# Graph layer with adjacency masks: products for two units at a time, one row step, the first x ahead of the first adjacency unit

## The reference

```python
masks = (relation[None] == rel_ids[:, None, None, None])      # rel_ids = 1..4
h = einsum('rbnm,bmd->rbnd', masks, x)
y = einsum('rbnd,rdo->bno', h, weight) + bias
out = layernorm(x + y, axis=-1, eps=1e-5)
```

## Time and profile before

| | |
|---|---|
| median of 3 runs | 120.71 us |
| the profiled execution | 120.54 us |
| its span, first to last instruction | 118.8 us |
| TensorE clock granted, mean | 0.985 |
| busy: PE, weight load, DVE, ACT, POOL | 106.6, 80.4, 84.8, 88.1, 70.3 us |
| 32 checks (L522) | 1994 ns each |
| 64 masks (L699) | 687 ns each |
| weight loads of the products (L619) | 98 ns each |
| x_lo on POOL (L448), one batch | 2144 ns |
| one row normalised on POOL (L488) | 457 ns |
| combining one row of statistics (L717) | 154 ns |
| DMA | 42.22 MB, mean 355 GB/s |

### The profile page before, as it was taken

How to read it: one execution, slowest core, us unless ns; L and a number is a source line. 1 busy time by engine, 2 the same in 40 slices (tenths; PEclk the granted TensorE clock), 3 DMA queues, 4 the chain that set the end, 5 groups by cost and what they waited for, 6 DMA issues and landing times.

```text
span 118.8 us, 2879 instructions
## 1 busy us (share of the span) xinstructions
PE 106.6 (90%) x1012; PEld 80.4 (68%) x1023; DVE 84.8 (71%) x252; ACT 88.1 (74%) x114; POOL 70.3 (59%) x132
## 2 busy tenths in 40 slices
PE   6788999899999979999999999999999999999400
PEld 2168898799997646767676767676868676679300
DVE  1055678397877848696959887787779777998840
ACT  4088277947797999799999499968987698925530
POOL 2007001940047998399569955995689577977740
PEclk9999999999999999999999999999999999999985
DMA  3999999999999999999999999999999999450271
GB/s 73 389 408 411 414 407 422 414 391 412 425 414 384 419 403 436 380 414 414 419 391 404 422 406 394 420 406 423 377 433 411 415 399 383 141 177 0 85 248 35
DMA packets 12419, 42.22 MB, mean 355 GB/s; under 512 B 882, under 2 KB 7155, under 8 KB 8947
## 3 DMA queue, kind: packets, MB, share of 16 engines
q1 hardware_dynamic: 12256, 41.49, 88.6%
q10 hardware_dynamic: 146, 0.52, 1.3%
HBM read 37.81 MB, written 4.19 MB: 354 GB/s over the span
## 4 chain that ended last, share of the span: by engine, by line
PE 58%; DMA 29%; SPq 5%; DVE 2%; issue 1%; ACT 0%; DVEq 0%
PE h_ps L619 32%; DMA adj_sb<-adj 29%; PE ids_t L601 16%; PE y_ps L633 9%; SPq L396 4%; PE ids_t L633 1%; DVE x_sb L758 0%; SPq L393 0%; SPq L412 0%; ACT std L539 0%; DVE stats L711 0%; DVE x_sb L705 0%; DVE moments L717 0%; DVEq L255 0%; DVE shift L751 0%
## 5 line engine op out<-in xcount | busy, mean ns | idle before, releaser
L522 ACT ACTIVATE junk<-adj_sb,minus 128x2048 bf16<-128x2048 int32 x32 | 63.8, 1994 | 0.4 <-DMA adj_sb<-adj 0.4
L699 DVE TENSOR_SCALAR mask_t<-ids_t 128x1024 bf16<-128x1024 uint16 x64 | 43.6, 687 | 25.2 <-PE ids_t L601 24.1
L601 PEld LDWEIGHTS ids_t<-ident,adj_sb 128*128 128x128 bf16 x512 | 36.5, 123 | 13.8 <-DMA adj_sb<-adj 2.7
L601 PE MATMUL ids_t<-ident,adj_sb 128*128 128x128 bf16 x512 | 40.0, 221 | 2.3 <-DMA adj_sb<-adj 2.2
L619 PE MATMUL h_ps<-mask_t,x_lo 128*128 128x512 bf16 (+2 forms) x184 | 33.5, 314 | 0.0
L619 PE MATMUL h_ps<-mask_t,x_hi 128*128 128x512 bf16 (+2 forms) x173 | 31.1, 310 | 1.2 <-DVE mask_t L699 0.6
L448 POOL TENSOR_TENSOR x_lo<-x_sb,x_hi 128x1024 f16<-128x1024 f32 x7 | 15.0, 2144 | 24.2 <-ACT x_hi L531 24.2
L488 POOL TENSOR_SCALAR x_sb<-x_sb,rstd,shift 128x128 f32<-128x128 f32 x55 | 24.0, 457 | 1.0
L535 ACT ACTIVATE h_all<-h_ps 128x512 f32<-128x512 f32 (+2 forms) x23 | 10.6, 463 | 18.1 <-PE h_ps L619 18.1
L454 POOL TENSOR_TENSOR x_sb<-x_sb,bias_sb 128x1024 f32<-128x1024 f32 x8 | 19.0, 2377 | 7.8 <-DVE x_lo L764 7.7
L619 PEld LDWEIGHTS h_ps<-mask_t,x_hi 128*128 128x128 f16 x184 | 15.6, 98 | 7.2 <-DVE mask_t L699 1.2
(11 more groups left out here) (44 smaller groups left out, 30.8 us busy)
## 6 DMA issues: line engine op xcount, KB each, us to landing
adj_sb<-adj SPq DMA_DIRECT2D x27, 1024.0 KB, 19.5
...
bias_row<-bias ACTq DMA_DIRECT2D x1, 0.5 KB
```

The costliest lines, as they stand in the source:

```text
L522: nc.scalar.activation(junk[:, at % 2], adj_sb[:, slot, 2 * k:2 * k + 2, :], ACT.Square, scale=2.0, bias=minus[:, 0:1], accum_out=squares[ ...
L601: last = nc.tensor.transpose(bank[:, j, :], words[:, j // step(b), j % step(b), 0, :], ident[:, :])
L699: nc.vector.tensor_scalar(mask_t[:, b % 2, :, u * P:(u + 1) * P], ids_t[u % T_BANKS][:, :, :].bitcast(UINT16), 1.0, None, ALU.mult).then_i ...
```

## The change

- Every batch but the last is split into groups of four units. Products are issued for two units at a time (256 columns), first with x_hi, then with x_lo; in batch 0's first group for one unit at a time. Transposes run between them: in a group's first half those of its own third and fourth unit, in its second half the first two of the next group. The group before is projected after the first half. The last batch stays 4, 2, 1, 1.
- All batches have row step 2. Batch 1 is loaded in single units.
- x of batch 0 is loaded by SP's queue, in two halves ahead of unit 0; ACT's queue only has the bias row. x of later batches moves ahead of the last pair of the batch before.
- DVE's and ACT's orders are rewritten for it. DVE sums the group one back. ACT checks two pairs a group (three in two groups) and makes x_hi after the first check.
- End: x is added to the last unit's projection on PE, by a product with an fp32 identity (`add_x`); its statistics and its normalising read PSUM. Only the rows that ACT normalises have a shift. Of the rows of the last 16 units POOL normalises 3 + 2 + 2 (4 + 2 + 1 before), ACT 5 + 2 (4 + 2 + 1), DVE the last 2.
- The second pass is rewritten in short loops over single units.

```diff
-    def step(b):
-        return J if b < EARLY else 2
+    S = 2
...
-        if b == 0:
-            return [(0, 1), (1, 1), (2, 2), (4, 2), (6, 2)]
-        if b == 1:
-            return [(0, 2), (2, 2), (4, 2), (6, 2)]
         return [(0, 4), (4, 2), (6, 1), (7, 1)] if b == B - 1 else [(0, 4), (4, 4)]
...
-        return b == 0 or (b == 1 and u < 2)
+        return b < EARLY
...
-        first = [1, 2, 2, 3, 4, 5, 6, 7, 8, 11, 13]
+        first = [2, 4, 6, 8, 10, 12, 15]
         if g.index < len(first):
             return first[g.index]
-        return min(PAIRS * (g.b + 1) + (2 if ends_batch(g) else 0), PAIRS * B)
+        return min(2 * g.index + 4, PAIRS * B)
...
+            for n in range(2):
+                sp.dma_start(units_of(x_sb[:, 0], n * HALF, HALF), rows_of(x, 0, n * HALF, HALF)).then_inc(s_x0[n], 16)
             load_unit(0, 0)
             load_unit(0, 1)
             sp.dma_start(w_sb[:, 0, :], weight[0]).then_inc(s_w, 16)
             for u in range(2, J):
                 load_unit(0, u)
-            load_unit(1, 0)
             load_x(1)
-            load_unit(1, 1)
-            for k in range(1, PAIRS):
-                load_adj(1, k)
-            load_x(2)
+            for u in range(J):
+                if u == 6:
+                    load_x(2)
+                load_unit(1, u)
             for b in range(EARLY, B):
                 for k in range(PAIRS):
+                    if k == PAIRS - 1 and b + 1 < B:
+                        load_x(b + 1)
                     load_adj(b, k)
-                if b + 1 < B:
...
-            normalise(full, full.units[:4])
+            normalise(full, full.units[:3])
             roots(ra)
             normalise(ra, ra.units[:2])
-            normalise(rb, rb.units[:1])
+            normalise(rb, rb.units[:2])
...
-            act.dma_start(units_of(x_sb[:, 0], 0, 0, J), rows_of(x, 0, 0, J)).then_inc(s_x[0], 16)
             act.dma_start(bias_row[:, :], bias.rearrange("(a d) -> a d", a=1)).then_inc(s_bias, 16)
             act.preload_act_table(ACT.Sqrt)
-            split_hi(0, slice(0, HALF), s_hi0)
-            split_hi(0, slice(HALF, J), s_hi)
+            split_hi(0, slice(0, HALF), s_x0[0], s_hi0)
+            split_hi(0, slice(HALF, J), s_x0[1], s_hi)
+            act.wait_ge(s_const, 1)
+            check(0, 0)
             act.wait_ge(s_spread, 1)
             nc.scalar.activation(bias_sb[:, :], y_ps[:, 0, :], ACT.Copy).then_inc(s_biased, 1)
-            act.wait_ge(s_const, 1)
-            check(0, 0)
+            check(0, 1)
             for g in groups[1:LAST]:
-                b = g.b
                 copy_h(groups[g.index - 1])
-                if ends_batch(g):
-                    split_hi(b + 1, slice(0, J), s_hi)
-                todo = range(pairs_checked_by(groups[g.index - 1]), pairs_checked_by(g))
-                for n, at in enumerate(todo):
+                for n, at in enumerate(range(pairs_checked_by(groups[g.index - 1]), pairs_checked_by(g))):
                     check(at // PAIRS, at % PAIRS)
-                    q = groups[g.index - 2] if g.index >= 2 else None
-                    if n == 0 and q and ends_batch(q):
-                        root(sets[q.b])
+                    if n == 0 and ends_batch(g):
+                        if g.b:
+                            root(sets[g.b - 1])
+                        else:
+                            continue
+                        split_hi(g.b + 1, slice(0, J), s_x[g.b + 1], s_hi)
+                if g.index == 1:
+                    split_hi(1, slice(0, J), s_x[1], s_hi)
...
-            normalise(full, full.units[4:5])
+            normalise(full, full.units[3:4])
             copy_h(e)
             root(ra)
-            normalise(full, full.units[5:7])
+            normalise(full, full.units[4:6])
             copy_h(d)
-            normalise(full, full.units[7:]).then_inc(s_aside, 1)
+            normalise(full, full.units[6:]).then_inc(s_aside, 1)
             root(rb)
             normalise(ra, ra.units[2:]).then_inc(s_aside, 1)
-            normalise(rb, rb.units[1:2]).then_inc(s_aside, 1)
...
-            def products(g, n, of):
-                todo = [(j, part) for part in (x_hi, x_lo) for j in range(J)]
-                lo, hi = len(todo) * n // of, len(todo) * (n + 1) // of
-                if n == 0:
-                    pe.wait_ge(s_mask, unit_no(g.b, g.units[-1]) + 1)
+            def products(g, units, part):
+                if part is x_hi:
+                    pe.wait_ge(s_mask, unit_no(g.b, units[-1]) + 1)
                     if g.index:
                         pe.wait_ge(s_hi, g.b + 1)
-                    if g.index >= 2:
+                    if g.index >= 2 and units[0] == g.first:
                         pe.wait_ge(s_h, g.index - 1)
-                if lo <= J < hi and g.index:
+                elif g.index:
                     pe.wait_ge(s_lo, g.b + 1)
-                for j, part in todo[lo:hi]:
-                    if g.index == 0 and j % HALF == 0:
+                to = slice((units[0] - g.first) * P, (units[-1] + 1 - g.first) * P)
+                cols = slice(units[0] * P, (units[-1] + 1) * P)
+                for j in range(J):
+                    if g.index == 0 and units[0] == 0 and j % HALF == 0:
                         pe.wait_ge(((s_hi0, s_hi) if part is x_hi else (s_lo0, s_lo))[j // HALF], 1)
-                    last = nc.tensor.matmul(h_ps[g.bank][:, 0:g.count * P], part[:, g.b % 2, j, :],
-                                            mask_t[:, g.b % 2, j, g.cols], start=(j == 0 and part is x_hi),
-                                            stop=(j == J - 1 and part is x_lo))
-                if hi == len(todo):
+                    last = nc.tensor.matmul(h_ps[g.bank][:, to], part[:, g.b % 2, j, :], mask_t[:, g.b % 2, j, cols],
+                                            start=(j == 0 and part is x_hi), stop=(j == J - 1 and part is x_lo))
+                if part is x_lo and units[-1] == g.units[-1]:
                     last.then_inc(s_prod, 1)
...
+            def add_x(g):
+                pe.wait_ge(s_whole, 1)
+                pe.wait_ge(s_xb, g.b + 1)
+                nc.tensor.matmul(y_of(g)[:, 0, :], whole_ident[:, :], x_sb[:, g.b, g.first, :], start=True, stop=False)
...
-            idle_turns(9)
+            idle_turns(11)
             pe.wait_ge(s_ident, 1)
             transpose_unit(0, 0)
+            idle_turns(2)
+            g = groups[0]
+            products(g, g.units[0:1], x_hi)
+            products(g, g.units[0:1], x_lo)
+            transpose_unit(0, 1)
             pe.wait_ge(s_const, 1)
             pe.wait_ge(s_bias, 16)
             nc.tensor.matmul(y_ps[:, 0, :], row_of_ones[:, :], bias_row[:, :], start=True, stop=True).then_inc(s_spread, 1)
-            idle_turns(2)
-            g = groups[0]
-            products(g, 0, 2)
-            transpose_unit(0, 1)
-            products(g, 1, 2)
-            g = groups[1]
-            products(g, 0, 2)
-            transpose_unit(0, 2)
-            project(groups[0])
-            products(g, 1, 2)
-            transpose_unit(0, 3)
-            for g in groups[2:LAST + 1]:
-                coming = coming_after(g)
-                for n, u in enumerate(coming):
-                    transpose_unit(groups[g.index + 1].b, u)
-                    if n == (len(coming) - 1 if g.index < LAST else 1):
+            for u in g.units[1:]:
+                transpose_unit(0, u + 1)
+                for part in (x_hi, x_lo):
+                    products(g, [u], part)
+            transpose_unit(0, GU + 1)
+            for g in groups[1:LAST + 1]:
+                n = groups[g.index + 1]
+                for units, coming in ((g.units[:2], [(g.b, u) for u in g.units[2:]]),
+                                      (g.units[2:], [(n.b, u) for u in n.units[:2]])):
+                    transpose_unit(*coming[0])
+                    products(g, units, x_hi)
+                    transpose_unit(*coming[1])
+                    products(g, units, x_lo)
+                    if units[0] == g.first:
                         project(groups[g.index - 1])
-                    products(g, n, len(coming))
             a, c, e, d = groups[LAST:]
-            products(c, 0, 2)
+            transpose_unit(e.b, e.first)
+            products(c, c.units, x_hi)
+            transpose_unit(d.b, d.first)
             project(a)
-            products(c, 1, 2)
-            products(e, 0, 1)
+            products(c, c.units, x_lo)
+            products(e, e.units, x_hi)
+            products(e, e.units, x_lo)
             project(c)
-            products(d, 0, 1)
-            project(e)
             pe.wait_ge(s_found, 1)
             nc.tensor.matmul(ids_t[0][0:1, 0, 0:2].bitcast(FP32), found[:, :], ones[:, :],
                              start=True, stop=True).then_inc(s_count, 1)
+            products(d, d.units, x_hi)
+            products(d, d.units, x_lo)
+            project(e)
```

(68 more changed lines are left out.)

261 lines of the change are left out of this document (108 added, 153 removed).

## The result

The changed kernel takes a median of **123.65 us** (123.43 to 124.03, 4 runs) beside 120.61 of the kernel before (120.49 to 120.75) on the same chip: ratio 1.0255, 95% interval 1.0224 to 1.0285. The forecast was 119.9, range 119.1 to 121.5. Where the executions of a kernel fall into a faster and a slower group, its median is that of all of them, and its ratio that of the means of the faster group. The profiled execution has a span of 122.0 us, where 118.0 was forecast.

A forecast was written before the change was run, and what follows sets the result against it. Loads bound the kernel first, then PE from about 40.7 us. Loop end gains 1.1, shrinking to 0.5 in the tail; with the tail's other terms 0.8 less: 120.71 - 0.8 = 119.9 us, range 119.1 to 121.5.

The forecast's parts named there:

- T22: Start on PE of the transpose of unit 22, counted from 0 over all batches; forecast 40.70 us.
- GpSimd's other form of normalising: Last rows on POOL: subtract and multiply priced like the old multiply and add, 0.44 a row, 0.1 either way.
- The anchor: Batch 2's pair 3 lands at 40.70 just as PE reaches it; from there PE is the limit, ten groups remain.
- rival (b): x in front fails: stream starts 0.5 later, ACT's three checks stall PE once for 0.3; 120.7 us, chance 0.16.
- The group, 6.25: PE's work for four units in the loop: 6.25 us, 0.06 more than before; low 6.19, high 6.35.
- Rival (d): Halved products cost more: 16 added weight loads a group uncovered, 1.6 us a group, 136 us; chance 0.01.
- Hand-over of masks: PE's products wait for DVE's mask of the unit just transposed; DVE may come 0.4 late, no stall forecast.
- ACT in the loop: ACT's copies, checks and x_hi in PE's groups: three checks leave cover of 0.1; price if gone 0.3.
- rival (a): Mask hand-over bites: DVE 0.6 late once a group, PE loses 10 x 0.2; 121.9 us, chance 0.23.
- The order of the tail: Steps of PE, DVE, ACT and POOL after the loop: last row 10.2 us after loop end, at 113.4.
- Store, landing and exit behind it: From the last row to the span's end: 4.6 us, taken as unchanged.
- The weighed rule of the Trainium skill: Fixed 2 us a transfer, 1 MiB or more advised: four added transfers, up to 8 us; forecast took none.

The follow-up runs named there:

- step8_x_whole_act: Changed kernel with POOL's old multiply-add form, row step 8 in batches 0 and 1, batch 0's x whole on ACT's queue: 117.77 us, 0.9789; again 118.12, 0.9782.
- shift_form: Changed kernel with POOL normalising every row by rstd and shift (multiply, add) as before: 120.33 us, 0.9929 of the kernel before.
- before_mean_form: Kernel before, with POOL normalising by mean and rstd (subtract, multiply): 127.09 us, 1.0530 of the kernel before.
- start_as_before_tail3: start_as_before with the last four rows shared among three engines as in the kernel before: 118.47 us, 0.9832 of the kernel before.
- start_as_before: step8_x_whole_act with batch 1 also loaded as in the kernel before (units 0 and 1 alone, then pairs): 118.37 us, 0.9822.

## Why the prediction was wrong, by its own steps

Span forecast 118.0, measured 122.0: loop end +2.5 (105.72 for 103.2; T22 +3.3, the ten groups -0.7), tail +3.4 (13.56 for 10.2), behind it -1.9 (2.7 for 4.6).

- **The tail, "GpSimd's other form of normalising ... taken as its nearest row, 0.1 either way": the step that failed most.** The nearest row was the other form (457 ns). An operation that the trace did not show was priced at one that it did, without a bound: it measures 783 to 801. POOL had 70 of 119 us busy, so there seemed to be room, but a batch takes POOL 2.15 for x_lo, 1.4 for the root, 2.38 for the bias and now 6.26 for rows, 12.2 of the 12.35 that PE needs. In the tail, where POOL is asked for rows and the bias at once, it has no such room. None of the rivals named POOL.
- **The anchor, "both meet ... 40.70", with "I take nothing; bounds -0.3 and +0.6" for the stream.** It came 3.3 late in the changed kernel and 0.2 and 0.7 late in the two executions of step8_x_whole_act. The mechanism was right, as PE starts unit 22 within 0.05 of its landing in all three; the size of one term was wrong: the head of the stream. By 14 us 0.73 MB were missing, with x in halves and in pieces of 1 KB; by the ratios x in one transfer and the old row step give back 1.7 us on ACT's queue (0.9789 for 0.9929) and 2.4 on SP's (0.9728). The row of the stores, 389 against 410 GB/s, is one of a full queue at the end; from 1 to 6 us the loads ran at 198 GB/s, where they had run at 280. "The bytes up to unit 1 are the same" was true and did not help; rival (b) had the sign and 0.5 of the 2.5 us by which the loop ended late. "PE's last wait for a load near 40.7" came as one of 1.43 at 31.22, for unit 14, and none that shows as idle time at 43.96.
- **"The first transpose stays [at 6.42] within 0.3"**: 7.48, and 8.43 in shift_form.
- **The group, 6.25**: 6.17, better than forecast. Products of 256 columns cost nothing more, and the projection, now ahead of a narrower product, takes 0.89 to its next step in place of 0.95. Rival (d) is out.
- **Hand-over of masks, ACT in the loop**: right, one wait of 0.3 at 17.7 us and none behind it; rival (a) fell.
- **The order of the tail**: right to 0.1 once POOL's form is mended (10.3 for 10.2, shift_form).
- **"Store, landing and exit behind it ... stay" (4.6)**: 2.7 in the changed kernel. In the profiled execution of before, from 116.2 us to the end only this is left of the stores (packets, MB, share of the engines' time):

```profile
q1 hardware_dynamic: 34, 0.03, 5.2%
```

34 packets that trickle in up to 117.8. before_mean_form, with the same stores, has 2.9, and start_as_before_tail3, where the last two stores again follow closely on each other, 3.2. What makes the 1.9 us stays open; no run was made for it.
- **The weighed rule of the Trainium skill.** DMA: Bandwidth & Descriptors gives a fixed cost of about 2 us for a transfer (Anatomy of one DMA — SWDGE (gpsimd) path) and advises 1 MiB or more (Bandwidth, Measured), both for transfers that GpSimd issues; those here are issued by SP and ACT, and the forecast named only the second place. I had written that the trace disagrees. For a full queue it does still: batch 1 in single units of 0.5 MB is no slower than in pairs (0.9789 for step8_x_whole_act, 0.9822 for start_as_before). For x at the head the rule had the sign: with pieces of 1 KB, one transfer is 0.8 us better than two halves. That is not its 2 us.

That shift_form lands on the forecast (0.9929 x 120.71 = 119.85) proves nothing: its loop end is 2.2 late and its end 1.9 early, and the two cancel.
